# Starting the expert loop on three token tiles while the last tile's rows are finished

## The chip, the cores and the metric

The kernel runs on one core of a Trainium2 chip. The metric is the device time of one execution in microseconds, the median over several runs. The engines are TensorE (PE), VectorE (DVE), ScalarE (ACT), GpSimd (POOL) and SyncE (SP), which here only issues DMAs.

## The reference

The input is x, 32 sequences of 56 tokens and 128 channels, with a context of 32 x 1500 x 128. The block has two residual parts:

```python
x = x + tanh(g_xattn) * attention(layernorm(x), ctx)      # 16 heads of depth 8, softmax over 1500 keys
x = x + tanh(g_ffn)   * ffn(layernorm(x))

# ffn, T = 1792 tokens, 160 experts with 64 inner channels
probs   = sigmoid(x @ router_w.T + expert_bias)
top_w   = top_k(probs, 8); top_w = 2.5 * top_w / (sum(top_w) + 1e-9)
combine = zeros(T, 160) with top_w at the chosen experts
h1      = silu(einsum('th,eih->eti', x, w_gate))
routed  = einsum('eti,ehi->th', h1 * combine.T[:, :, None], w_down)
shared  = silu(x @ w_gate_shared.T) @ w_down_shared.T
ffn     = routed + shared
```

Every expert is computed for every token, and the combine weights (zero for experts not chosen) are multiplied in.

## The kernel before

**Layout.** A row of 112 tokens (PT) is the same position of two sequences; there are 16 such rows (NP). Four rows make a token tile of 448 tokens (TC), and there are four tiles (NTC). Two experts form a pair of 128 inner channels; there are 80 pairs (EP).

**Attention.** It runs over 32 batches in software-pipelined steps of 12 slots. Step s works on the keys of batch s, the maxima of batch s-1, the scores and the value products of batches s-2 and s-3, and finishes batch s-3. Slots, step numbers and named places (TOKENS_AT, LOGITS_AT, COMBT_AT and so on) order the work by hand, and each engine executes its own list in order. SyncE issues the context loads, the transposing DMAs, the stacking of keys (L387) and the row q_st (L405). GpSimd splits the context into a high and a low half-precision part (L495, L497), makes q_blk (L585) and q_st (L603), and prepares two or three expert pairs per step: load (L468 twice, L470), split (L512 to L516), store to w_scratch (L518). The 80 pairs are done when attention ends. When two batches are through, TensorE multiplies by the output weights (L1263) and VectorE adds the result to one row of xt (L1007). So the rows become ready one by one, and the last one only behind the last batch.

**Router.** Rows 0 to 11 are normalised on GpSimd in step 32, transposed, and multiplied by the router weights while attention ends. ScalarE applies one sigmoid to them (L723), VectorE finds the eight largest and clears them in a copy (L981, L984), and forms the combine weights (L988 to L994) for all twelve rows. TensorE transposes them (L1320), VectorE copies them (L959), SyncE stores them to c_scratch (L428) and reads them back, spread over 64 partitions for each expert of a pair (L421). For the last four rows, the tile 3, the same is done after the last batch, with nothing of the expert loop beside it but the shared expert's up products and the first pair's.

**Expert loop.** For each pair and tile: three up products of high and low parts (L1340), silu (L778), a product with the combine weights (L1066, "weighing"), the high part (L784), the low part (L1072) and three down products (L1368) into an accumulating bank. YB are the four banks that accumulate, ZB the four that take up products. ScalarE's order is silu of a unit, then the high part of the unit before it; VectorE's is weighing of a unit, then the low part of the unit before it; TensorE's is the down product of the unit four back (the same tile), then the up product. The intermediate values are h_f, h_hi and h_lo with a place for each tile, and s_act with two places. Expert weights (w_ring, by a transposing DMA, L439) and combine weights (c_ring) are rings of four pairs. The first four pairs are written out, the others run in a loop of 19 turns. The end (L802, L1391, L1090) transposes back, adds the residual and stores.

## Time and profile before

| | us |
|---|---|
| median of 3 runs | 1140.1 |
| lowest and highest | 1139.61, 1145.44 |
| profiled execution, its own time | 1140.58 |
| its span | 1139.1 |
| PE, DVE, ACT, POOL busy | 1069.6, 969.8, 845.1, 610.7 |

The profile lists the busy time of each engine, and for each group of instructions what ended the idle time before it. The timeline views give the start of an instruction in microseconds from the span's start, its duration, engine, line, operation and the tiles it writes and reads; in square brackets stands the idle time of its engine just before it and what ended it. "SPq" is the issuing of DMAs by SyncE. "issue" means that the profile shows nothing that was waited for. The windows view gives busy times in stretches of the span, with the clock granted to TensorE as a share of full speed (1.00 is 2.4 GHz, 0.50 is 1.2 GHz), the DMA engines' busy share and what they moved.

### The profile page before, as it was taken

What the parts mean: (1) busy time and instruction counts of PE and PEld (TensorE: products, weight loads), DVE (VectorE), ACT (ScalarE), POOL (GpSimd) and SP (SyncE); (2) the same over time, 40 slices, a digit from 0 to 9 for tenths busy, and PEclk for the clock granted to TensorE, in tenths of its full rate; (3) what the DMA queues carried; (4) which work ended last, traced back from release to release, by engine and by line L of the source; (5) the groups of instructions that cost most, each with busy time, mean ns of one, the idle gap of its engine ahead of it and who ended that gap; (6) DMA issues with size and microseconds to landing.
All of it is one profiled execution on the core that took longest, in us unless ns stands there. A gap on an engine that the chain in (4) does not pass through costs nothing.

```text
span 1139.1 us, 37969 instructions
## 1 busy us (share of the span) xinstructions
PE 1069.6 (94%) x12090; PEld 708.6 (62%) x12090; DVE 969.8 (85%) x1706; ACT 845.1 (74%) x1812; POOL 610.7 (54%) x1042
## 2 busy tenths in 40 slices
PE   2798899999999999999999999879999999999998
PEld 1366677777777777777777777644555555555554
DVE  3677788888888888888888888669999999999998
ACT  2566577777777777767777776658888888888886
POOL 4887888888888888888888988000000000000000
PEclk9799999999999999999999999889999999999999
DMA  6786866757667767568577552146777767776673
GB/s 129 162 179 150 187 155 171 170 137 182 154 143 184 156 161 176 135 159 180 139 182 164 132 144 61 25 138 209 231 226 232 239 227 226 234 236 226 225 240 115
DMA packets 201816, 197.06 MB, mean 173 GB/s; under 512 B 161999, under 2 KB 168207, under 8 KB 201782
## 3 DMA queue, kind: packets, MB, share of 16 engines
q1 hardware_dynamic: 188292, 174.14, 58.2%
q0 software_dynamic: 11520, 20.99, 6.5%
q10 hardware_dynamic: 1970, 1.49, 0.7%
q8 instruction: 18, 0.29, 0.1%
q14 instruction: 16, 0.13, 0.0%
HBM read 109.96 MB, written 12.55 MB: 108 GB/s over the span
## 4 chain that ended last, share of the span: by engine, by line
PE 45%; POOL 21%; issue 16%; DVE 9%; SPq 3%; DMA 2%; POOLq 2%; ACT 1%; DVEq 0%; ACTq 0%
PE bank L1368 15%; PE bank L1340 15%; PE bank L1170 4%; PE bank L1184 4%; DVE part_max L897 3%; POOL ctx_parts L495 3%; PE bank L1203 3%; POOL q_st L603 3%; POOL q_blk L585 3%; POOL w_in L468 3%; POOL w_in L470 2%; POOL w_out L516 2%; POOL w_out L515 2%; DVE rec L1024 2%; PE bank L1239 2%
## 5 line engine op out<-in xcount | busy, mean ns | idle before, releaser
L701 ACT ACTIVATE p_exp<-bank 125x448 f32<-125x448 f32 x768 | 400.2, 544 | 193.4 <-PE bank L1184 192.4
L897 DVE TENSOR_REDUCE part_max<-bank 128x1 f32<-128x500 f32 x672 | 420.9, 672 | 71.6 <-PE bank L1203 71.2
L1184 PE MATMUL bank<-q_st,k_stk 97*125 97x224 f16 x1536 | 275.6, 264 | 15.5 <-DMA q_st<-neg_row 8.9
L1203 PE MATMUL bank<-kparts,q_blk 128*128 128x500 f16 x672 | 256.3, 385 | 13.4 <-DVE part_max L897 11.2
L1184 PEld LDWEIGHTS bank<-q_st,k_stk 97*125 97x125 f16 x1536 | 197.2, 139 | 80.3 <-ACT p_exp L701 16.4
L1368 PE MATMUL bank<-ctT,w_ring 128*128 128x448 f16 x960 | 234.0, 353 | 3.0 <-DVE ctT L1072 3.0
L778 ACT ACTIVATE ctT<-bank 128x448 f32<-128x448 f32 x320 | 173.6, 543 | 40.6 <-PE bank L1340 16.1
L1072 DVE TENSOR_TENSOR ctT<-k_stk,ctT 128x448 f16<-128x448 f32 x320 | 198.2, 619 | 0.5 <-ACT ctT L784 0.4
L1170 PE MATMUL bank<-p_exp,v_sb 125*25 125x168 f32 (+1 forms) x6144 | 187.9, 263 | 0.4 <-ACT p_exp L701 0.4
L784 ACT ACTIVATE ctT<-k_stk 128x448 f16<-128x448 f32 x320 | 181.7, 568 | 5.5 <-DVE k_stk L1066 3.2
L1340 PE MATMUL bank<-q_hi,w_ring 128*128 128x448 f16 x640 | 174.0, 354 | 2.4 <-ACT k_stk L767 2.4
L1170 PEld LDWEIGHTS bank<-p_exp,v_sb 125*25 125x25 f32 x6144 | 142.9, 104 | 43.5 <-issue 0.6
L1066 DVE TENSOR_TENSOR k_stk<-v_sb,ctT 128x448 f32<-128x448 f32 x240 | 149.6, 624 | 8.3 <-DMA v_sb<-c_scratch 3.3
L1368 PEld LDWEIGHTS bank<-ctT,w_ring 128*128 128x128 f16 x960 | 91.5, 97 | 93.3 <-DVE ctT L1072 22.8
L497 POOL TENSOR_TENSOR ctx_parts<-ctx_in,ctx_parts 128x512 f16<-128x512 f32 x96 | 112.6, 1172 | 8.0
L1340 PE MATMUL bank<-q_lo,w_ring 128*128 128x448 f16 x320 | 113.0, 353 | 0.0
L1340 PEld LDWEIGHTS bank<-q_hi,w_ring 128*128 128x128 f16 x640 | 62.5, 98 | 61.8 <-issue 2.6
L1015 DVE SCALAR_TENSOR_TENSOR kparts<-bank,bkc,kparts 128x500 f16<-128x500 f32 x93 | 68.1, 732 | 36.3 <-ACT kparts L756 36.3
L1203 PEld LDWEIGHTS bank<-kparts,q_blk 128*128 128x128 f16 x672 | 64.8, 97 | 39.1 <-DVE part_max L897 20.3
L468 POOL DMA_DIRECT2D w_in<-in_L_ffn_w_gate_dram x160 | 85.8, 537 | 5.7
L1239 PE MATMUL bank<-wv_hi,ctT 128*125 128x128 f16 x768 | 85.0, 225 | 0.0
L1239 PEld LDWEIGHTS bank<-wv_hi,ctT 128*125 128x125 f16 x768 | 78.7, 142 | 2.9 <-issue 2.8
(157 smaller groups left out, 1241.1 us busy)
## 6 DMA issues: line engine op xcount, KB each, us to landing
v_sb<-c_scratch SPq DMA_DIRECT2D x114, 448.0 KB, 4.0
k_stk<-kparts SPq DMA_DIRECT2D x384, 93.8 KB, 3.5
ctx_in<-in_ctx_dram SPq DMA_DIRECT2D x30, 672.0 KB
k_stk<-c_scratch SPq DMA_DIRECT2D x38, 448.0 KB, 3.9
w_scratch<-w_out POOLq DMA_DIRECT2D x80, 128.0 KB, 3.2
w_in<-in_L_ffn_w_gate_dram POOLq DMA_DIRECT2D x160, 32.0 KB, 3.3
w_in<-in_L_ffn_w_down_dram POOLq DMA_DIRECT2D x80, 64.0 KB, 3.4
ctx_in<-in_ctx_dram SPq DMA_DIRECT2D x30, 78.0 KB
```

The source lines that it names most:

```text
L701: act.activation(p_exp[0:KP, j % PR, f * 448:(f + 1) * 448], ST[f][0:KP, 0:448], ACT.Exp).then_inc(exp_done, 1)
L778: act.activation(s_act[:, t % 2, :], ZB[t][:, 0:TC], ACT.Silu).then_inc(s_done, 1)
L784: act.activation(h_hi[:, t, :], h_f[:, t, :], ACT.Copy).then_inc(hh_done, 1)
L897: v.reduce_max(part_max[:, i // NCH, i % NCH:i % NCH + 1], SM[i % NSM][:, 0:CK], axis=AX.X).then_inc(sm_maxed, 1)
L1066: v.tensor_tensor(h_f[:, t, :], c_ring[q][:, t * TC:(t + 1) * TC], s_act[:, t % 2, :], ALU.mult).then_inc(h_done, 1)
L1072: v.tensor_tensor(h_lo[:, t, :], h_f[:, t, :], h_hi[:, t, :], ALU.subtract).then_inc(hl_done, 1)
L1170: last = pe.matmul(OB[32 * (g % 4):32 * (g % 4) + VW, at:at + w], v_sb[0:KP, u, j, g, 0:VW], p_exp[0:KP, j % PR, src:src + w], start=(j == ...
L1184: last = pe.matmul(ST[f][0:KP, (g % 2) * GC:(g % 2 + 1) * GC], k_stk[0:97, u, g, j * KP:(j + 1) * KP], q_st[0:97, u, g, :, :].rearrange("p ...
L1203: pe.matmul(SM[i % NSM][:, 0:CK], rows, kparts[:, u, 0, c * CK:(c + 1) * CK], start=True, stop=True).then_inc(sm_done, 1)
L1239: last = pe.matmul(VB[0:KP, i * D:(i + 1) * D], ctT[:, u, c, part, i, 0:KP], w[:, :], start=(n == 0), stop=(n == 2))
L1340: last = pe.matmul(ZB[t][:, 0:TC], w_ring[:, q, a, :], xparts[b][:, t * TC:(t + 1) * TC], start=(j == 0), stop=(j == 2))
L1368: last = pe.matmul(YB[t][:, 0:TC], w, hparts[b][rows, t, :], start=(shared and i == 0), stop=(end and i == 2), skip_group_check=True)
```

## The change

Units are numbered k in the order in which they are started. The first three are the shared expert for tiles 0 to 2. Then come 24 units: eight expert pairs (AHEAD) for tiles 0 to 2 (TS is 3). Unit 27 (TAIL) is the shared expert of tile 3, and units 28 to 35 are the same eight pairs for tile 3. From unit 36 on the order is as before, from pair 8.

In the 27 first units h_f, h_hi, h_lo and the up banks have three places in use, and GpSimd makes the low parts in place of VectorE. In between, at fixed unit numbers, stands what was done for tile 3 before: the last residual row behind unit 5, three Newton steps on VectorE in place of ScalarE's root, the scaling, tokens at 12, logits at 15, sigmoid, the eight largest, the weights, and their transposes at 24. The last batch's spread and output products move from the last attention step into this list.

The router's work for tiles 0 to 2 is done tile by tile: searches and sums on VectorE, the subtraction and the product with the sum's inverse on GpSimd. TensorE gets twelve products without use (keep_busy) where ScalarE computes the sigmoid. SyncE loads the eight pairs' expert weights (w_ahead) before the combine weights; it stores and reads back the combine weights tile by tile (two pairs per DMA for the first four pairs), and tile 3's for all eight pairs by two DMAs (c_last). c_ring is laid out by tile, so a load writes four pieces to each partition. h_f lies in xnT. The gate matrices of a pair are loaded by one DMA in place of two, and the early normalisation has three Newton rounds in place of four. YB, ZB, TOKB, LGB and CTB get other banks.

```diff
+    AHEAD, TS = 8, NTC - 1
+    TAIL = TS + TS * AHEAD
+    OUT_LATE, TOKENS_LATE, LOGITS_LATE, COMBT_LATE = 5, 12, 15, 24
...
+        c_last = e_words[:, 0:AHEAD * TC].rearrange("p (n c) -> p n c", c=TC)
...
-        YB = [bank[0], bank[1], bank[2], bank[3]]
-        ZB = [bank[4], bank[5], bank[6], bank[7]]
+        YB = [bank[0], bank[1], bank[5], bank[4]]
+        ZB = [bank[7], bank[2], bank[3], bank[6]]
...
+        def earlier(k):
+            if k < TS or k == TAIL:
+                return 0
+            return k - TS + 1 if k < TAIL else k - NTC + 1
...  SyncE
+            def store(c):
+                sp.wait_ge(cb_cp, 2 * c + 2)
+                sp.dma_start(c_scratch[:, :, c * TC:(c + 1) * TC], combT[0:EP, :, c * TC:(c + 1) * TC]).then_inc(c_stored, 16)
+                sp.wait_ge(c_stored, 16 * (c + 1))
...
+            for n in range(AHEAD):
...
+                sp.dma_start_transpose(w_ahead[n], w_scratch[n].rearrange("p b c -> p (b c)")).then_inc(w_first, 16)
...
+            for t in range(TS):
+                store(t)
+                for j in range(2):
+                    for a in range(2):
+                        src = c_scratch[2 * j:2 * j + 2, a, t * TC:(t + 1) * TC].unsqueeze(0).to_broadcast([I, 2, TC])
+                        sp.dma_start(c_pairs[j][a::2, t, :, :], src).then_inc(c_first[t], 16)
...
+            for n in range(WR, AHEAD):
+                sp.wait_ge(h_done, TS * (n - WR) + TS)
+                weights_of(n, n % WR, TS)
+            store(TS)
+            sp.wait_ge(pv_done, B * KT)
+            for a in range(2):
+                src = c_scratch[0:AHEAD, a, TS * TC:N].unsqueeze(0).to_broadcast([I, AHEAD, TC])
+                sp.dma_start(c_last[a::2, :, :], src).then_inc(c_late, 16)
...  GpSimd
             def load_pair(h, i):
-                for a in range(2):
-                    pool.dma_start(w_in[a::2, i, 0, :], gate_pairs[bass.ds(h * WPP + i, 1), a].rearrange("a p c -> p (a c)"))\
-                        .then_inc(w_here[i], 16)
+                pool.dma_start(w_in[:, i, 0, :], gate_pairs[bass.ds(h * WPP + i, 1)].rearrange("a e p c -> p (a e) c"))\
+                    .then_inc(w_here[i], 16)
...
+            for k in range(TAIL):
+                b = k % TS
+                rows = slice(0, I if k < TS else 128)
+                pool.wait_ge(hh_done, k + 1)
+                until(pool, dn_done, earlier(k))
+                pool.tensor_tensor(h_lo[rows, b, :], h_f[rows, b, :], h_hi[rows, b, :], ALU.subtract).then_inc(hl_done, 1)
...  ScalarE
+            for k in range(TS, TAIL):
+                silu(k, k % TS, weighed(k))
+                if k > TS:
+                    hi_part(k - 1, (k - 1) % TS, weighed(k - 1), earlier(k - 1))
+                if k == TOKENS_LATE + 1:
+                    tokens(TS)
+                if k == LOGITS_LATE + 3:
+                    sigmoid(2, *LATE)
...  VectorE, behind the eight pairs
+            dve.wait_ge(c_late, 32)
+            for k in range(TAIL + 1, TAIL + 1 + AHEAD):
+                weigh(k, place(k), weighed(k), c_last[:, k - TAIL - 1, :])
+                lo_part(k - 1, place(k - 1), I if k - 1 == TAIL else 128)
...  TensorE
+            def keep_busy():
+                pe.wait_ge(lg_biased, 2)
+                for _ in range(WARM):
+                    pe.matmul(bank[2][0:I, 0:TC], sg[:, 0, :], q_hi[:, 0:TC], start=True, stop=True)
...
+            for n in range(1, AHEAD):
+                for t in range(TS):
+                    k = TS + TS * n + t
+                    down(k - TS, t, t, w_ahead[n - 1])
+                    up(k, t, t, w_ahead[n])
+                    if k == TOKENS_LATE:
+                        tokens(TS)
+                    if k == LOGITS_LATE:
+                        logits((4, 5))
+                    if k == COMBT_LATE:
+                        weights_out(TS)
+            pe.wait_ge(cb_cp, 2 * NTC)
+            shared_up(TS)
```

## Rows read from the trace of the kernel before

**Rows 1.** Windows: stretch, its length, busy us (instructions) of each engine.
```profile
720.00:730.00 10.00, 9.27 (x89) 6.38 (x90) 5.22 (x31) 5.45 (x12) 0.00 (x0) 0.50 0.10 23
...
745.00:772.00 27.00, 18.57 (x76) 10.11 (x76) 17.39 (x49) 12.17 (x22) 0.00 (x0) 0.81 0.42 132
747.00:756.00 9.00, 7.41 (x30) 4.83 (x29) 4.44 (x16) 2.03 (x3) 0.00 (x0) 0.69 0.90 300
772.00:1130.00 358.00, 357.40 (x1888) 182.52 (x1889) 351.94 (x632) 317.80 (x631) 0.00 (x0) 1.00 0.69 224
```
The engines are PE, PE's weight loads, DVE, ACT and POOL; then follow the granted clock, the DMA engines' share and GB/s.

**Rows 2.** Timeline of TensorE, two of its waits in attention.
```profile
131.28 0.40 PE L1184 MATMUL bank<-q_st,k_stk 97*125 97x224 f16 x2 [3.03 <-DMA q_st<-neg_row]
...
508.09 0.40 PE L1184 MATMUL bank<-q_st,k_stk 97*125 97x224 f16 x2 [1.08 <-DMA q_st<-neg_row]
```

**Rows 3.** Timeline of GpSimd in attention.
```profile
379.63 1.67 POOL L585 TENSOR_TENSOR q_blk<-q_hi,head_mask 128x896 f16<-128x896 f16 x1
...
392.25 1.12 POOL L468 DMA_DIRECT2D w_in<-in_L_ffn_w_gate_dram  x2
393.37 0.71 POOL L470 DMA_DIRECT2D w_in<-in_L_ffn_w_down_dram  x1
...
420.91 1.67 POOL L585 TENSOR_TENSOR q_blk<-q_hi,head_mask 128x896 f16<-128x896 f16 x1
...
471.84 0.71 POOL L470 DMA_DIRECT2D w_in<-in_L_ffn_w_down_dram  x1 [2.34 <-issue]
...
473.25 1.16 POOL L497 TENSOR_TENSOR ctx_parts<-ctx_in,ctx_parts 128x512 f16<-128x512 f32 x1
```

**Rows 4.** Timeline of VectorE: o_nrm, once in each step.
```profile
432.28 0.39 DVE L1028 TENSOR_TENSOR o_nrm<-rec,o_raw 128x224 f32<-128x224 f32 x1
...
473.62 1.04 DVE L1028 TENSOR_TENSOR o_nrm<-rec,o_raw 128x224 f32<-128x224 f32 x1
...
516.90 0.65 DVE L1028 TENSOR_TENSOR o_nrm<-rec,o_raw 128x224 f32<-128x224 f32 x1
```

**Rows 5.** Timeline of all engines late in the expert loop.
```profile
1122.08 0.73 PE L1368 MATMUL bank<-ctT,w_ring 128*128 128x448 f16 x3
...
1122.28 0.54 ACT L778 ACTIVATE ctT<-bank 128x448 f32<-128x448 f32 x1
...
1122.72 0.57 ACT L784 ACTIVATE ctT<-k_stk 128x448 f16<-128x448 f32 x1
...
1122.97 0.62 DVE L1066 TENSOR_TENSOR k_stk<-v_sb,ctT 128x448 f32<-128x448 f32 x1
1123.03 0.35 PE L1340 MATMUL bank<-q_lo,w_ring 128*128 128x448 f16 x1
```

**Rows 6.** Timeline of ScalarE and TensorE at the end of attention.
```profile
715.17 1.28 ACT L723 ACT_TABLE_LOAD   x1
...
720.18 1.07 PE L1184 MATMUL bank<-q_st,k_stk 97*125 97x224 f16 x4 [3.67 <-ACT p_exp L701]
...
742.83 0.59 PE L1170 MATMUL bank<-p_exp,v_sb 125*25 125x168 f32 x16 [0.36 <-ACT p_exp L701]
```

**Rows 7.** DMA issues: engine, count, KB each, median us to landing.
```profile
v_sb<-c_scratch SPq DMA_DIRECT2D x6, 336.0 KB, 5.3
c_scratch<-q_stk SPq DMA_DIRECT2D x4, 280.0 KB, 3.0
...
v_sb<-c_scratch SPq DMA_DIRECT2D x6, 112.0 KB, 2.8
```

**Rows 8.** Timelines of SyncE, VectorE and TensorE before the dense stretch.
```profile
745.32 3.76 SPq L421 DMA_DIRECT2D v_sb<-c_scratch  x6
...
763.56 1.14 DVE L959 COPY q_stk<-bank 80x448 f32<-80x448 f32 x2
...
771.16 0.63 DVE L1066 TENSOR_TENSOR k_stk<-v_sb,ctT 128x448 f32<-128x448 f32 x1 [3.25 <-DMA v_sb<-c_scratch]
...
772.38 0.74 PE L1368 MATMUL bank<-ctT,w_ring 128*128 128x448 f16 x3 [2.80 <-DVE ctT L1072]
```

465 lines of the change are left out of this document (268 added, 197 removed).

## The prediction, made before the result was known

> **What bounds the kernel now.** I read four views in this order. First the busy time by stretches [rows 1]. The reader is to see that from 772 to 1130 us TensorE is busy 357.4 of 358.0 us at a granted clock of 1.00: the expert loop is bound by TensorE. From 745 to 772 it is busy only 18.6 of 27 us, at 0.81. The change aims at this second stretch, and at what lies just ahead of it.
>
> Then the timelines, to find which wait ends last at the edges. In the attention loop TensorE has three waits for the row of q_st, of which the first and the last stand in [rows 2]. That row is sent only when GpSimd has made q_st. GpSimd [rows 3] never idles there: from one q_blk to the same one two steps later it takes 41.28 us (379.63 to 420.91). TensorE's own two steps take 41.34 (432.28 to 473.62 in [rows 4]). So GpSimd has almost no slack. When its DMA issue hangs for 2.34 us at 471.84, the next two steps take 43.28 us instead of 41.34.
>
> The expert loop deals in units: the up product, silu, weighing, hi part, lo part and down product of one token tile for one expert pair. There are 324 (80 pairs and the shared expert, times four tiles). One costs TensorE six products. At 772.4 [rows 8] 316 are left, and the stretch to 1130.5 gives 1.133 us each [rows 1]. So I count units: the change is worth what it finishes before the dense stretch, less what it adds.
>
> **1. Attention loop: one gate DMA for two.** For each expert pair two issues of together 1.12 us become one of 128 rows. It costs between 0.56 (one of the two) and 0.71 us (the down matrices' issue, also over 128 partitions) [rows 3]. GpSimd gains 0.41 to 0.56 per expert pair, 2.0 to 2.8 per two steps, so the hangs of about 2.3 us are swallowed. These cost 1.9 us at 473.62 to 516.90 [rows 4] and about 1.1 at the one before. In the first wait of [rows 2] the three expert pairs ahead of it give 1.7, and the two before them let the preceding step begin 0.4 earlier: 2.1 of 3.03 us go, and with them the half clock from 132.8 to 136, worth 1.6. Sum 6.6; I take **-6.0**. The bounds are -7.5 (all three waits and the clock) and -3.0 (hangs only). TensorE is otherwise busy, so nothing more comes. One Newton round less saves GpSimd four small operations that nobody waits for: 0.
>
> **2. Last steps of attention.** Probabilities need two table loads of 1.28 us, TensorE idles 3.67 us, and then runs at half clock from 720 to 730 [rows 1, 6]. Twelve added products of 0.19 us fill 2.3 us of that idle time, for nothing, since they end before the scores' banks are freed. At full clock the stretch would be bound by ScalarE's exponentials. I take **-2.4** (bounds 0, if the clock falls all the same, and -4.6, half of the 9.27 us busy). The router's two long products leave VectorE for idle GpSimd; VectorE's searches are the same in number. The last value product ends about 741.0 instead of 743.4 [rows 6].
>
> **3. Start of the eight pairs.** SyncE handles the tiles one after another: store (3.0 us to landing), wait, four loads at 0.63 each [rows 7, 8]: 5.5 us, and the issue of the store. From about 731.3 these rounds put the loads of tile 2 at 745.3 to 747.8, and they land near 750.7. The units of tiles 0 and 1 don't need them; the first weighing of tile 2 waits until 750.7. Its w_ahead transposes stand before 727 and are hidden. Without this wait TensorE would be ready about 748, so 2 to 3 us hang on it.
>
> **4. Rate of the eight pairs.** Here I see the main cost. With three tiles a ring closes: an up product, silu of k, then hi of k-1 (behind silu of k on ScalarE), lo of k-1 on GpSimd, its down product, and the up product of k+2. From [rows 5]: 0.04 to silu, 1.01 for silu and hi, 1.30 from the start of a down to the end of the up behind it. GpSimd's subtraction of 512 columns takes 1.16 [rows 3]; 448 columns are about 1.03. With 0.08 for each of two handovers the ring is 0.04 + 1.01 + 0.08 + 1.03 + 0.08 + 1.30 = 3.54 us for two units: **1.77 per unit**, not 1.133. Bounds: 1.133 (TensorE alone) and 2.35 (the same ring with TensorE's 1.30 at half clock).
>
> VectorE's late work (row 15, Newton, tokens, logits, top 8) lies in the slack of about 1 us per unit; I charge only the burst behind the first tile-2 unit. ScalarE's sigmoid with two table loads of 1.28 [rows 6] is about 3.3 us, less 0.75 of slack; for TensorE's logits and transposes I estimate 0.9. The up product of unit 8 ends at 754.4 and that of unit 11 at 760.4; fourteen units at 1.77 and the 3.5 extra give 788.7 for unit 25.
>
> The SBUF lock is the skill's rule against this part. At 473.62 o_nrm, two SBUF inputs, takes 1.04 instead of 0.39 us and ends with GpSimd's subtraction that began at 473.25 [rows 3, 4]. The Trainium skill (SBUF — State Buffer, Who interferes with whom) says that a VectorE instruction with two SBUF inputs and a GpSimd one that reads SBUF exclude each other. By it weighing (0.62) and lo would be in series, but in this ring lo starts when weighing ends, so it would add 0.05 per unit, about 1 us in all, plus 1 or 2 where a late product gets in first.
>
> **5. Tile 3 catches up.** The wait of before for tile 3's weights (3.25 us, [rows 8]) comes back larger. VectorE's two copies of the transposed weights (1.14, [rows 8]) end about 790.9. Then the store, 3.1 with its issue; then two loads of 8 x 448 words to 64 partitions each, 1.83 MB. Loads ran at 300 GB/s in 747 to 756 [rows 1], 6.1 us for these, and took 1.7 from the issue at 745.3 [rows 8] to the first bytes: 7.8 (bounds 5.3, one 336 KB load [rows 7], and 10). They land at 801.8. Only units 26 and 28 to 30 are in flight meanwhile: TensorE stops at about 795. Queued behind the waiting weighing of unit 28 is the lo part of unit 27, and for that waits down 27. It starts 1.2 later, at **803.0**.
>
> By the Trainium skill (DMA: Bandwidth & Descriptors, Anatomy of one DMA), 2.0 us plus bytes over 436 GB/s, an estimate for these loads would be 6.2 instead of 7.8, and the sum 1.6 lower; the trace's rate is the lower one.
>
> **6. Dense stretch.** At 803.0, when down 27 starts, 297 downs and 293 ups remain, 295 units. Before, at 772.4, there were 318 and 314, 316 units. The end moves by 803.0 - 772.4 - 21 x 1.133 = **+6.8**. After 8 us of idleness the clock will be low at the restart, as it was at 720: I take 3.4 us at half rate, **+1.7** (bounds 0 and 4.6). The loads of the combine weights now write four pieces of 1792 bytes instead of one of 7168; the nearest rows are small and large loads of before, at 2.8 and 5.3 us [rows 7], while a slot is refilled some three pairs (13.6 us) ahead: 0, hidden by TensorE, and up to +10 if DMA became the bound, which I hold unlikely. New banks: 0, none is shared by two streams.
>
> **Sum.** On the clock of the profile parts 2 to 5 are inside the 803.0. So 1140.58 + 6.8 + 1.7 - 6.0 = 1143.1 for the profiled execution, which stood 0.5 above the median of 1140.1 (its span is 1139.1, 1.5 lies outside). I predict **1142.5**, no difference that can be told: a measurement of this kernel tells 0.5% (5.7 us) from none.
>
> **The rivals.** (a) *TensorE, not the ring, paces the eight pairs.* If silu, hi and lo hide as in the four-tile loop, the 17 units from 8 to 25 save 0.64 each, 10.9 us, and the time is 1142.5 - 10.9 = 1131.6. For it: in [rows 5] every handover is 0.04 to 0.1, and matmul ends are modelled. Against it: the order on ScalarE and a GpSimd subtraction nearly twice VectorE's 0.62. A part of it (1.5 per unit) and the short end of the loads would already give 1136.
>
> (b) *The clock falls in the eight pairs* (slower). In the ring TensorE is busy 1.13 of 1.77, 64%. For it: 745 to 772 was granted 0.81 at 18.6 of 27 us, 69% busy [rows 1]. Against: gaps of 0.6 us are short beside the 3.67 ahead of 720. At half clock throughout the unit is 2.35, 17 x 0.58 = +9.9: 1152.4. It decides if more than a third of that stretch is at half clock.
>
> (c) *The merged gate DMA changes nothing*, because TensorE's waits have another cause (the row's own DMA): +6.0, 1148.5. For it: the releaser named in [rows 2] is a DMA. Against: that DMA is issued right behind q_st.
>
> **How the numbers follow.** As worked out 0.42, (a) in whole or part 0.30, (b) 0.15, (c) 0.13. The first gives no difference in 0.34 and a faster or slower kernel in 0.04 each, its own range is 1136 to 1149. (a) is faster in 0.27 and the same in 0.03; (b) and (c) are slower in 0.25, the same in 0.03. So faster 0.31, same 0.40, slower 0.29. The range, 1130 to 1153, reaches to (a) and (b) whole; about 0.15 is left out.
>
> **What would show it.** Part 1: no wait for q_st's row at 131, 299 and 508, two steps at 41.3 throughout, GpSimd with idle time. Part 2: PEclk 1.0 from 720 to 745. Part 4: downs 1.77 apart between the first and the last of the eight pairs. Part 5: a wait of VectorE for the weights of tile 3 of 8 to 10 us, TensorE idle 8, a low clock behind it. Part 6: from the end of the wait to the end 295 x 1.133 us. I am wrong if the eight pairs run near 1.3 per unit, or if the stall on tile 3's weights is under 4 us.

## The result: slower by 1.5%, outside the range

| | before | after |
|---|---|---|
| median, us | 1139.9 (4 runs) | 1157.9 (4 runs) |
| lowest and highest | 1139.51, 1145.44 | 1156.26, 1159.31 |
| ratio, with its 95% interval | | 1.0149 [1.0129, 1.0169] |
| profiled execution, its span | 1140.58, 1139.1 | 1156.67, 1155.1 |

The forecast was 1142.5, in a range of 1130 to 1153: 15.4 us too low. In the profiled executions the miss is 13.6 (1156.67 against the sum of 1143.1). Line numbers below are those of the changed kernel: L1301 value products, L1490 up, L1500 down, L1157 weighing, L1166 and L672 lo on VectorE and GpSimd, L831 hi, L825 silu, L1110 o_nrm.

The windows of the profile after (same columns as [rows 1]) show at once where the time is not:

```profile
738.00:749.00 11.00, 8.12 (x43) 3.96 (x41) 4.19 (x5) 6.24 (x13) 4.89 (x5) 1.00 0.37 119
749.00:762.00 13.00, 7.52 (x20) 2.58 (x21) 7.29 (x22) 2.82 (x6) 3.65 (x4) 0.51 0.62 165
762.00:783.00 21.00, 15.84 (x78) 7.19 (x76) 10.38 (x18) 14.10 (x26) 10.76 (x10) 0.98 0.31 99
783.00:790.00 7.00, 5.32 (x14) 1.92 (x15) 5.14 (x20) 3.04 (x8) 3.51 (x3) 0.52 0.00 0
790.00:800.00 10.00, 6.66 (x36) 3.19 (x35) 7.10 (x9) 5.10 (x11) 5.76 (x5) 1.00 0.00 0
800.00:815.00 15.00, 7.67 (x32) 3.21 (x31) 4.46 (x8) 4.86 (x11) 1.29 (x2) 0.77 0.87 309
815.00:1130.00 315.00, 315.00 (x1667) 162.69 (x1665) 309.88 (x555) 280.15 (x556) 0.00 (x0) 1.00 0.77 224
```

From 815 TensorE is full, as it was from 772 before. The loss lies between 738 and 815: 77 us in which TensorE is busy for 51.1, part of it at half clock. A summary of waits over this stretch (engine, line, what it waited for, us in total, times, longest) names the places:

```profile
DVE xnT L1157 <- ACT ctT L825: 13.4, 9, 3.7
DVE xnT L1157 <- DMA p_exp<-c_scratch: 9.9, 1, 9.9
DVE xnT L1157 <- DMA k_stk<-c_scratch: 9.3, 2, 5.9
...
PE bank L1500 <- POOL ctT L672: 14.4, 12, 4.1
PE bank L1500 <- DVE ctT L1166: 7.3, 1, 7.3
```

The waits for DMAs are those for the weights of tiles 1 and 2 (k_stk from c_scratch, 3.3 and 5.9 us) and of tile 3 (p_exp); the others belong to the ring of three tiles and to what gets in its way. Cut at the events that the prediction had placed:

| stretch | forecast | after | off |
|---|---|---|---|
| to the last value product | 735.0 | 737.75 | +2.75 |
| from there to the first weighing of tile 2 (753.46) | 9.7 | 15.7 | +6.0 |
| from there to the end of up(25) (796.57) | 38.0 | 43.1 | +5.1 |
| from there to down 27 (810.53) | 14.3 | 14.0 | -0.3 |
| from there to the end | 344.6 | 344.6 | 0.0 |

(The forecast's 803.0 for down 27 and the times ahead of it are moved by its -6.0 of part 1.) The first row flatters the forecast: TensorE's first wait, for the loaded Wo, happened to be 3.4 us shorter in this execution than in that of before (10.87 and 14.29). Without that, parts 1 and 2 missed by some 6 us, not 2.75.

**Tile 2's weights.** SyncE's queue: start, duration of the issue, what is issued.

```profile
728.96 0.69 SPq L446 DMA_DIRECT2D c_scratch<-q_stk  x1
732.00 1.38 SPq L464 DMA_DIRECT2D v_sb<-c_scratch  x2
...
734.72 0.64 SPq L446 DMA_DIRECT2D c_scratch<-q_stk  x1
741.07 1.27 SPq L464 DMA_DIRECT2D v_sb<-c_scratch  x2
...
743.68 0.62 SPq L446 DMA_DIRECT2D c_scratch<-q_stk  x1
747.67 1.26 SPq L464 DMA_DIRECT2D v_sb<-c_scratch  x2
```

Each first load is issued when the store before it has landed. The stores took 3.04, **6.35** and 3.99 us, where I had taken 3.0 from [rows 7] for all three. The two late ones were issued right behind four loads; in [rows 7] the stores had no load ahead of them. Eight further kernels below have the same chain of stores: their first store took 3.0 to 3.1 us, the second 3.9 to 6.0, the third 3.8 to 4.1. So a store behind loads always took longer, and 6.35 was the longest of nine. From the first store's issue to the first weighing of tile 2 it is 24.5 us (728.96 to 753.46) where the forecast had 19.4 (731.3 to 750.7): 5.1 of the 6.0.

**VectorE held up.** Timeline rows of VectorE, GpSimd and TensorE at the end of attention, and of VectorE in the eight pairs:

```profile
719.51 1.53 POOL L663 TENSOR_TENSOR ctx_in<-kparts,ctx_in 112x640 f32<-112x640 f32 x1 [0.76 <-DVE ctx_in L1057]
719.56 1.51 DVE L1063 TENSOR_SCALAR wsum<-wsum 112x4 f32<-112x4 f32 x1
721.39 0.39 DVE L982 COPY o_raw<-bank 128x224 f32<-128x224 f32 x1
...
721.93 1.52 PE L1301 MATMUL bank<-p_exp,v_sb 125*25 125x168 f32 x24 [2.35 <-DVE o_raw L982]
...
758.29 0.99 DVE L1130 TENSOR_TENSOR lst<-lst 112x4 f32<-112x4 f32 x1
...
761.03 0.15 DVE L1130 TENSOR_TENSOR lst<-lst 112x4 f32<-112x4 f32 x1
```

An addition to four numbers a row took 1.51 us (1.51 or 1.52 in each of the three tiles; before the change such additions took 0.17), and ended when GpSimd's subtraction of 640 columns did. The two rows of L1130 are the same instruction, a product of four numbers a row in row 15's Newton steps, once beside GpSimd's lo and once not: 0.99 and 0.15. Two of row 15's later pieces were held up in the same way: its scalings (L1137) took 1.31 us for two, and the subtraction for its combine weights (L1145) 1.68. In e10 and e13 below, where GpSimd makes no lo there, the three take 0.15, 0.60 and 0.82. TensorE's wait at 721.93 is the third in that chain.

**The ring.** TensorE's down products where nothing late is in the way:

```profile
763.98 0.74 PE L1500 MATMUL bank<-ctT,ctx_parts 128*128 128x448 f16 x3 [0.53 <-POOL ctT L672]
...
765.75 0.74 PE L1500 MATMUL bank<-ctT,ctx_parts 128*128 128x448 f16 x3 [0.46 <-POOL ctT L672]
```

They are 1.77 us apart, as forecast, and so are the next three. ScalarE then loads the sigmoid's table and silu's again, and TensorE finds itself at half clock behind it:

```profile
779.16 1.28 ACT L783 ACT_TABLE_LOAD   x1
...
781.21 1.28 ACT L825 ACT_TABLE_LOAD   x1
...
784.68 1.30 PE L1500 MATMUL bank<-ctT,ctx_parts 128*128 128x448 f16 x3 [3.03 <-POOL ctT L672]
```

**Tile 3** waits nearly as forecast (9.9 us of VectorE, 7.33 of TensorE; the same wait before is in [rows 8]):

```profile
801.89 1.29 SPq L477 DMA_DIRECT2D p_exp<-c_scratch  x2
...
809.32 0.63 DVE L1157 TENSOR_TENSOR xnT<-p_exp,ctT 128x448 f32<-128x448 f32 x1 [9.91 <-DMA p_exp<-c_scratch]
...
810.53 1.30 PE L1500 MATMUL bank<-ctT,sd 64*128 64x448 f16 x3 [7.33 <-DVE ctT L1166]
```

### The profile page after: what moved, and what is told of

Same layout as the page of the kernel before. It is cut to its first block, busy times and chain, and to the rows that moved or that the text cites. A ratio compares the mean times of both kernels' runs of the same rounds, so it can differ in the third digit from the quotient of the medians.

```text
span 1155.1 us, 37333 instructions
## 1 busy us (share of the span) xinstructions
PE 1072.5 (93%) x12102; PEld 708.9 (61%) x12102; DVE 965.2 (84%) x1695; ACT 845.5 (73%) x1810; POOL 613.2 (53%) x991
## 4 chain that ended last, share of the span: by engine, by line
PE 73%; DVE 11%; issue 5%; SPq 4%; POOL 3%; DMA 3%; ACT 1%; DVEq 0%; POOLq 0%
PE bank L1500 15%; PE bank L1490 15%; PE bank L1301 11%; PE bank L1334 10%; PE bank L1315 10%; DVE part_max L968 6%; PE bank L1370 4%; PE bank L1358 4%; DVE rec L1106 3%; POOL ctT L672 1%; PE bank L1413 1%; SPq L412 1%; SPq L367 1%; DMA ctx_in<-in_ctx_dram 1%; SPq L359 1%
## 5 line engine op out<-in xcount | busy, mean ns | idle before, releaser
L825 ACT ACTIVATE ctT<-bank 128x448 f32<-128x448 f32 x320 | 173.9, 544 | 57.0 <-PE bank L1490 24.0
L1500 PE MATMUL bank<-ctT,w_ring 128*128 128x448 f16 x864 | 210.6, 352 | 0.1
L831 ACT ACTIVATE ctT<-xnT 128x448 f16<-128x448 f32 x320 | 182.1, 569 | 20.2 <-DVE xnT L1157 17.7
L1301 PE MATMUL bank<-p_exp,v_sb 125*25 125x168 f32 (+1 forms) x6144 | 186.7, 262 | 2.3 <-DVE o_raw L982 2.3
L1166 DVE TENSOR_TENSOR ctT<-xnT,ctT 128x448 f16<-128x448 f32 (+1 forms) x297 | 183.7, 619 | 0.1
L1301 PEld LDWEIGHTS bank<-p_exp,v_sb 125*25 125x25 f32 x6144 | 142.5, 104 | 44.6 <-issue 2.5
L1490 PE MATMUL bank<-q_hi,w_ring 128*128 128x448 f16 x576 | 156.0, 352 | 0.0
L1500 PEld LDWEIGHTS bank<-ctT,w_ring 128*128 128x128 f16 x864 | 84.3, 98 | 79.1 <-DVE ctT L1166 3.8
L1157 DVE TENSOR_TENSOR xnT<-v_sb,ctT 128x448 f32<-128x448 f32 x156 | 97.2, 623 | 20.6 <-DMA k_stk<-c_scratch 9.3
L1157 DVE TENSOR_TENSOR xnT<-k_stk,ctT 128x448 f32<-128x448 f32 x156 | 98.1, 629 | 8.9 <-ACT ctT L825 5.6
L1490 PE MATMUL bank<-q_lo,w_ring 128*128 128x448 f16 x288 | 101.5, 352 | 0.0
L1097 DVE SCALAR_TENSOR_TENSOR kparts<-bank,bkc,kparts 128x500 f16<-128x500 f32 x93 | 68.0, 731 | 35.8 <-ACT kparts L816 35.8
L1334 PEld LDWEIGHTS bank<-kparts,q_blk 128*128 128x128 f16 x672 | 65.0, 97 | 41.3 <-DVE part_max L968 22.8
L1490 PEld LDWEIGHTS bank<-q_hi,w_ring 128*128 128x128 f16 x576 | 56.4, 98 | 52.7
```

The lines of the kernel that those rows point to most:

```text
L825: act.activation(s_act[:, (b if isinstance(r, int) is False else r - 1) % 2, :], ZB[b][:, 0:TC], ACT.Silu)\
L831: act.activation(h_hi[:, b, :], h_f[:, b, :], ACT.Copy).then_inc(hh_done, 1)
L1157: v.tensor_tensor(h_f[:, b, :], c, s_act[:, (b if isinstance(r, int) is False else r - 1) % 2, :], ALU.mult).then_inc(h_done, 1)
L1166: v.tensor_tensor(h_lo[0:rows, b, :], h_f[0:rows, b, :], h_hi[0:rows, b, :], ALU.subtract).then_inc(hl_done, 1)
L1301: last = pe.matmul(OB[32 * (g % 4):32 * (g % 4) + VW, at:at + w], v_sb[0:KP, u, j, g, 0:VW], p_exp[0:KP, j % PR, src:src + w], start=(j == ...
L1334: pe.matmul(SM[i % NSM][:, 0:CK], rows, kparts[:, u, 0, c * CK:(c + 1) * CK], start=True, stop=True).then_inc(sm_done, 1)
```

## The experiments

Each is timed as a ratio to the kernel before on the same chip; the changed kernel's is 1.0149. The intervals are some 0.2% to 0.4% to either side, so a difference of two ratios below 3 us (5 us for e9) is not settled by them, and the traces carry it. They are compared by three stretches, since executions of the same code already start differently: TensorE's first wait, for the loaded Wo, was 14.3 us in the profiled execution of before, 10.9 in that of after and 10.9 to 15.0 over all runs. OB is the bank in which the value products of attention add up; VectorE copies it once for each batch (o_raw<-bank). The columns are: from the last copy of OB to the first weighing of tile 2; from there to the first weighing of tile 3; from there to the end.

| kernel | ratio [95%] | copy to tile 2 | tile 2 to tile 3 | to the end |
|---|---|---|---|---|
| after | 1.0149 [1.0129, 1.0169] | 15.6 | 55.9 | 345.8 |
| e1_sums_first | 1.0138 [1.0102, 1.0175] | 15.6 | 56.3 | 346.0 |
| e4_store_queue | 1.0122 [1.0098, 1.0145] | 11.9 | 56.0 | 346.3 |
| e5_hi_first | 1.0176 [1.0149, 1.0203] | 14.6 | 58.9 | 346.9 |
| e6_two_loads | 1.0159 [1.0133, 1.0185] | 12.9 | 53.6 | 346.3 |
| e9_up_first | 1.0110 [1.0068, 1.0151] | 15.5 | 49.5 | 345.6 |
| e10_up_first_lo_vector | 1.0127 [1.0092, 1.0162] | 14.8 | 50.1 | 346.3 |
| e14_no_table | 1.0111 [1.0094, 1.0128] | 14.8 | 52.2 | 346.8 |
| e15_short_chain | 1.0072 [1.0055, 1.0089] | 13.9 | 49.0 | 344.3 |
| e12_all_lo_gpsimd | 0.9972 [0.9954, 0.9991] | 10.4 | 43.7 | 344.5 |
| e13_all_lo_vector | 0.9997 [0.9983, 1.0010] | 10.7 | 45.5 | 344.4 |
| f2_all_phase | 0.9995 [0.9983, 1.0006] | 10.2 | 43.5 | 344.0 |
| f3_no_busy | 1.0176 [1.0156, 1.0196] | 14.2 | 55.1 | 345.6 |

The second column repeats to within 1.2 us where the code in it is the same (55.1 to 56.3); the first does not (12.9 to 15.6), so a gain in it under 3 us is not shown. Most of that spread is the landing of tile 1's store: 3.9 us in e6, which has 12.9, and 6.35, 6.0 and 5.5 in after, e1 and e9, which have 15.5 to 15.6.

### e1_sums_first

```diff
-                then(pool.tensor_tensor(comb[:, p, :], prob[:, p, :], comb[:, p, :], ALU.subtract))
                 pool.wait_ge(sums_done, c + 1)
+                then(pool.tensor_tensor(comb[:, p, :], prob[:, p, :], comb[:, p, :], ALU.subtract))
```

> The changed kernel, but GpSimd waits for VectorE's sums before its first product of the combine weights (prob minus comb), not between its two products. Theory (the GpSimd product shuts out VectorE's small operation): the three 112x4 additions of VectorE's sums, 1.51 to 1.52 us each in the changed kernel against 0.17 before the change, go back to about 0.2; the copy of OB at 721.4 starts about 1.3 us earlier, TensorE's wait of 2.35 us at 721.9 shrinks to about 1 and the half clock behind it goes; the last value product ends 1.5 to 3 us earlier than 737.75, and the time falls by as much, from 1157.9 to 1155 to 1156.5. Rival (the small additions are long because the semaphore of the chain arrives late, or by another engine's traffic): they stay at 1.5 us and the time does not move. A second rival: GpSimd's product, now later, meets the next VectorE operation instead (search or copy), which then takes 1.2 to 1.5 us: same total.

Measured: 1157.75 us, ratio 1.0138. The additions in its trace:

```profile
717.50 0.17 DVE L1063 TENSOR_SCALAR wsum<-wsum 112x4 f32<-112x4 f32 x1
...
720.28 0.84 DVE L1063 TENSOR_SCALAR wsum<-wsum 112x4 f32<-112x4 f32 x1
```

The first is at 0.17; the other two (0.84 and, at 724.05, 0.54) now meet the end of GpSimd's second product of the tile before. So the product did hold the addition up. From o_nrm at 701.3 to the copy of OB at 721.5 it is 20.1 us against 22.1 in after: 2.0 us gained. (This stretch repeats: 22.1 in every variant of the changed kernel with the old order, 20.1 in every one with the new.) TensorE's wait of 2.35 is gone, but from the one copy of OB to the next it takes 18.2 instead of 16.4, because half clock lasted from 718 to 728 where it had been 722 to 725. (Other kernels with after's code show 16.5 to 17.8 here, so this is in part chance.) No gain in time is shown. The mechanism held; that the clock would give more on top was wrong.

### e4_store_queue

```diff
             for t in range(TS):
-                store(t)
+                if t == 0:
+                    store(t)
+                else:
+                    sp.wait_ge(c_stored2[t - 1], 16)
                 for j in range(2):
...
             for k in range(TS):
+                if k < TS - 1:
+                    act.wait_ge(cb_cp, 2 * k + 4)
+                    act.dma_start(c_scratch[:, :, (k + 1) * TC:(k + 2) * TC], combT[0:EP, :, (k + 1) * TC:(k + 2) * TC])\
+                       .then_inc(c_stored2[k], 16)
                 shared(k, k)
```

> The changed kernel, but the stores of the combine weights of tiles 1 and 2 are issued by ScalarE, behind its last exponential, in a queue of its own; SyncE only waits for them before the loads. Theory (the second and third store stand in SyncE's queue behind the loads of the tile before, and SyncE waits out each landing): the store of tile 1, 6.35 us from issue to landing in the changed kernel, takes about 3; the loads of tile 2 are issued by about 740 instead of 750.2, the wait of 5.93 us that VectorE has before the first tile-2 weighing (753.5) goes, this weighing starts near 748, and TensorE's low clock from 749 to 762 shortens. Time 4 to 7 us under the changed kernel's 1157.9, about 1152. Rival (the loads themselves set the time, their landing takes as long wherever the stores are): first tile-2 weighing within 1 us of 753.5, no gain. Second rival (the gain is given back at tile 3): the ring of the eight pairs starts 5 us earlier, but the late work of row 15 does not, and the wait for tile 3's weights grows by the same: time as it was.

Measured: 1155.5 us, ratio 1.0122. ScalarE's issues, and VectorE's first weighing of tile 2:

```profile
738.86 0.72 ACTq L849 DMA_DIRECT2D c_scratch<-q_stk  x1
...
741.77 0.59 ACTq L849 DMA_DIRECT2D c_scratch<-q_stk  x1
...
752.47 0.62 DVE L1165 TENSOR_TENSOR xnT<-v_sb,ctT 128x448 f32<-128x448 f32 x1 [2.39 <-DMA k_stk<-c_scratch]
```

Tile 1's store stands behind ScalarE's last exponentials and is issued at 738.9, not 734.7; it took 4.5 to landing and landed later than in after. Tile 2's landed by 745.9, and then all loads followed one another. The wait of 5.9 for tile 2 became 2.4. That is 3.7 us in the table's first column against after and 1.0 against the shortest of the same code, and none in the second: the rounds are a cost of their own, smaller than I expected from this way of mending it. And a queue of its own did not bring the store back to 3 us while loads were under way: 4.5 here, 5.3 in e12 below. That speaks for the transfers under way, and not only for its place in SyncE's queue; no run takes the two apart.

### e5_hi_first

```diff
             for k in range(TS, TAIL):
-                silu(k, k % TS, weighed(k))
                 if k > TS:
                     hi_part(k - 1, (k - 1) % TS, weighed(k - 1), earlier(k - 1))
+                silu(k, k % TS, weighed(k))
```

> The changed kernel, but in the loop of three tiles over eight pairs ScalarE makes the hi part of unit k-1 before silu of unit k, not behind it. Ring theory: the ring was silu and hi (1.01), GpSimd's lo (1.03), down and up (1.30) and the handovers, 3.54 us for two units, 1.77 each. In the new order one unit's own chain is up, silu 0.5, weighing 0.62, hi 0.5, lo 1.03, down and up 1.30 and handovers, 4.28 us for three units, 1.43 each. Down products 1.4 to 1.5 apart where they were 1.77, 17 units save 0.34 each: 5 to 6 us, less what the late burst on VectorE holds: the time falls from 1157.9 to 1152 to 1154. Rival (GpSimd and VectorE exclude each other on two SBUF inputs, so weighing 0.62 and lo 1.03 are in series at 1.65 us a unit whatever ScalarE's order): 1.65 to 1.7 per unit, a gain of 1 to 2 us. Second rival (TensorE's clock sets the rate): it stays at 1.77.

Measured: 1161.0 us, ratio 1.0176. The intervals touch, but the middle stretch is 3.0 us longer than in after. A unit took 2.20 us, and one turn of the ring reads (hi, lo, weighing, next hi):

```profile
771.71 0.58 ACT L831 ACTIVATE ctT<-xnT 128x448 f16<-128x448 f32 x1 [1.19 <-DVE xnT L1157]
...
772.36 1.04 POOL L672 TENSOR_TENSOR ctT<-xnT,ctT 128x448 f16<-128x448 f32 x1 [1.17 <-ACT ctT L831]
...
772.75 1.13 DVE L1157 TENSOR_TENSOR xnT<-k_stk,ctT 128x448 f32<-128x448 f32 x1 [1.07 <-ACT ctT L825]
...
773.91 0.58 ACT L831 ACTIVATE ctT<-xnT 128x448 f16<-128x448 f32 x1 [0.76 <-DVE xnT L1157]
```

The weighing starts at 772.75, lasts 1.13 instead of 0.62 and ends half a microsecond behind GpSimd's lo (773.40). The next hi needs it. So hi, lo and weighing form a ring although no semaphore joins lo to weighing. Without the hold-up the ring of hi, silu and weighing would be 1.7 us: my expectation of 1.43 had missed that ring too. Both my theory and its figure fell; the lock, given there as the first rival at 1.65 to 1.7, is real and costlier than I had put it.

### e6_two_loads

```diff
-            for a in range(2):
-                src = c_scratch[0:AHEAD, a, TS * TC:N].unsqueeze(0).to_broadcast([I, AHEAD, TC])
-                sp.dma_start(c_last[a::2, :, :], src).then_inc(c_late, 16)
+            for s, n0 in ((c_late, 0), (c_late2, AHEAD // 2)):
+                for a in range(2):
+                    src = c_scratch[n0:n0 + AHEAD // 2, a, TS * TC:N].unsqueeze(0).to_broadcast([I, AHEAD // 2, TC])
+                    sp.dma_start(c_last[a::2, n0:n0 + AHEAD // 2, :], src).then_inc(s, 16)
```

> The changed kernel, but tile 3's combine weights for the eight pairs are loaded in two halves (four pairs each, a semaphore each), and VectorE waits for the second half only before the fifth of its eight units. Theory (the stall of the catching-up tile is store, fixed time of a DMA, and bytes at some 300 GB/s): the first half lands 3.0 us earlier, 4.8 us behind the issue instead of 7.4; VectorE's wait of 9.9 us shrinks to about 7, TensorE's of 7.3 to about 4.5; time 2.5 to 4 us under 1157.9. Rival (the time to landing is mostly fixed, or halves of one queue share the engines): under 1 us. A wait for the second half may come back four units later: it has 3 x 1.13 us and the first unit to land in, so at most 1 us.

Measured: 1157.9 us, ratio 1.0159: no gain by the times; 2.3 us in the middle stretch of the trace. In its trace VectorE's wait is 7.80 where it was 9.91, and TensorE's 5.22 where it was 7.33:

```profile
806.96 0.62 DVE L1158 TENSOR_TENSOR xnT<-p_exp,ctT 128x448 f32<-128x448 f32 x1 [7.80 <-DMA p_exp<-c_scratch]
...
808.16 1.30 PE L1503 MATMUL bank<-ctT,sd 64*128 64x448 f16 x3 [5.22 <-DVE ctT L1167]
```

Halving the bytes saved 2.1 of 7.4 us from issue to landing, not 3.0, and half clock behind the wait stays. The stall is more fixed time than I had counted.

### e2_gate_only and e3_busy_only

The kernel before, with one part of the change alone. The first is the diff's load_pair and its count of 32 (part 1 of the prediction); the second adds twelve products (part 2):

```diff
+            def keep_busy():
+                pe.wait_ge(lg_biased, 2)
+                for _ in range(WARM):
+                    pe.matmul(bank[2][0:I, 0:TC], sg[:, 0, :], q_hi[:, 0:TC], start=True, stop=True)
```

> The kernel before the change with one part alone: the gate matrices of an expert pair come in one DMA of 128 rows, not in two of 64. The prediction gave this part -6.0 us (bounds -7.5 and -3.0). The trace of the changed kernel speaks for less: the early o_nrm came 5.0 us sooner (136.65 against 141.68), but the last value product only 5.6 sooner with another part in it, and two steps take 41.65 us throughout. Theory: the gain is made before 160 us and at the one hang, and a toll of 0.3 us per two steps (every second o_nrm takes 0.7 instead of 0.39 us and holds up the maxima behind it) gives part of it back over 13 pairs of steps: 1 to 3 us faster than before. Rival (the prediction as it stood): two steps at 41.34 throughout and 6 us faster. Second rival: nothing, because the early stretch differs from run to run by as much.

Measured: 1138.8 us in 10 runs, ratio 0.9981 [0.9963, 1.0000], that is -2.2 us (-4.2 to 0) for a forecast of -6.0. GpSimd's hangs no longer stop TensorE, but two steps take 41.65 to 41.7 us nearly throughout instead of 41.34. An o_nrm of every second step in its trace (those between take 0.39):

```profile
513.30 0.75 DVE L1027 TENSOR_TENSOR o_nrm<-rec,o_raw 128x224 f32<-128x224 f32 x1
```

From the third o_nrm (141.7 before, 137.7 here) to the one near 700 it takes 563.6 us, and 562.8 before: this toll of 0.3 us per two steps cancels what the hangs gave. What is left is the early stretch, 4.0 us, and 2.6 of these are TensorE's shorter first wait for Wo (11.65 for 14.29). The other traces agree. With the merged DMA the third o_nrm comes 0.9 to 3.9 us earlier behind that wait than before, and from there to the one near 700 it takes 562.3 to 563.6 us (565.9 in f2), against 562.8 and 563.3 in the two kernels without it.

> The kernel before the change with one part alone: twelve added products of TensorE behind the last early logits, while ScalarE makes the probabilities. The prediction gave -2.4 us for the clock from 720 to 730. Theory now: the granted clock still falls to 0.5, only later or earlier by a few us, as it did in the three last variants of the changed kernel (718 to 728 at 0.5 with these products in), because TensorE is slack in this stretch, not only idle once: time within 1 us of before. Rival (the prediction): PEclk 1.0 throughout 716 to 740 and 2 to 3 us faster.

Measured: 1140.9 us in 10 runs, ratio 1.0011 [0.9993, 1.0029]: no gain. Its windows:

```profile
720.00:730.00 10.00, 8.98 (x162) 6.08 (x160) 8.24 (x27) 7.00 (x16) 0.00 (x0) 1.00 0.03 6
...
766.00:774.00 8.00, 6.67 (x20) 2.82 (x21) 5.62 (x10) 3.71 (x8) 0.00 (x0) 0.57 0.42 99
```

The profile looks as the rival said, and the time is the theory's: full clock from 720 to 730 as in the prediction, and from o_nrm at 703.0 to the last copy of OB 35.8 us instead of 39.0. But from that copy to the end it takes 398.1 instead of 395.6: here the clock was low from 766 to 773, where the same window of before shows 1.00. (Before was low earlier, 0.58 from 760 to 764, where e3 shows 1.00.)

### e9_up_first and e10_up_first_lo_vector

```diff
                     k = TS + TS * n + t
-                    down(k - TS, t, t, w_ahead[n - 1])
                     up(k, t, t, w_ahead[n])
+                    down(k - TS, t, t, w_ahead[n - 1])
```

> The changed kernel, but in the loop of three tiles TensorE issues the up product of unit k before the down product of unit k-3, so that an up no longer waits behind a down for the lo part. This takes the up product out of the ring that I counted: up, silu, hi, lo, down would then close over three units, 3.54 / 3 = 1.18 us. Lock theory (GpSimd's lo, 1.03, and VectorE's weighing, 0.54 to 0.62, shut each other out, as in the run with hi first, where weighing took 1.12 us and a unit 2.20): they are in series, at least 1.65 us a unit whatever TensorE's order; down products 1.65 to 1.7 apart, the time 1 to 3 us under 1157.9. Rival (no lock, the ring alone): 1.2 to 1.3 per unit where VectorE has no late work, 8 to 10 us under 1157.9.

Measured: 1152.5 us, ratio 1.0110; tile 2 to tile 3 takes 49.5 instead of 55.9. The ring of TensorE is out of the way, and GpSimd and VectorE alternate (both rows are groups of instructions without idle time in between):

```profile
769.03 3.37 DVE L1157 TENSOR_TENSOR xnT<-k_stk,ctT 128x448 f32<-128x448 f32 x3
...
769.28 5.01 POOL L672 TENSOR_TENSOR ctT<-xnT,ctT 128x448 f16<-128x448 f32 x4 [1.30 <-PE bank L1500]
```

Three weighings in 3.37 us are 1.12 each, four lo parts in 5.01 are 1.25 each, where alone they take 0.62 and 1.03. The gain lies between theory and rival: the two engines hold each other up, but one lo and one weighing did not take the 1.65 us in series that I had expected.

The second kernel has this and the lo parts of the routed units on VectorE:

```diff
-            for k in range(TAIL):
+            for k in range(TS):
...
                     weigh(k, t, weighed(k), c_ring[n % WR][:, t, :])
+                    if k == TS + 1:
+                        dve.wait_ge(hl_done, TS)
+                    if k > TS:
+                        lo_part(k - 1, (k - 1) % TS)
```

> As the run before (up product ahead of the down product in the loop of three tiles), and the lo part of the routed units made by VectorE, as in the dense loop, so that GpSimd has nothing there. Lock theory: without GpSimd's products no weighing is held up, VectorE paces the loop at 1.12 to 1.2 us a unit where it has no late work, and the late work of row 15 (about 10 us on VectorE by its rows in the changed kernel) adds to it: 24 units in 37 to 39 us instead of 43, 4 to 6 us under 1157.9. TensorE at 1.13 of 1.2 us a unit should also keep its clock. Rival (the late chain on VectorE becomes the bound, since every piece of it now waits behind two products a unit, so that tile 3's weights come as late as before): stall for tile 3's weights longer by what the loop gained, time 1156 to 1159.

Measured: 1153.8 us, ratio 1.0127; 50.1 us in the middle stretch, wait for tile 3's weights 8.5. What VectorE gains by being free of GpSimd's products it gives back by making the lo parts itself.

### e14_no_table and e15_short_chain

```diff
-                act.activation(prob[:, p0:p1, :], prob[:, p0:p1, :], ACT.Sigmoid).then_inc(prob_done, 1)
+                act.activation(prob[:, p0:p1, :], prob[:, p0:p1, :], ACT.Sigmoid if n == 1 else ACT.Silu).then_inc(prob_done, 1)
```

> The changed kernel, but the late sigmoid (tile 3's probabilities, in the middle of the eight pairs) is replaced by Silu, whose table is loaded already: this leaves out the sigmoid of the last four rows of tokens, so their routing is another. Theory: the two table loads of 779.2 to 782.5 and TensorE's wait of 3.0 us at 784.7 go, and so does the half clock from 784 to 790; everything behind it, the late chain too, is earlier by 3.0 to 3.7 us for the wait and 1 to 2 for the clock: 1157.9 falls to 1153 to 1154. Rival (the ring has slack of 0.6 us a unit, so the stall is made up, or the wait for tile 3's weights grows by it): within 1 us of 1157.9.

Measured: 1153.2 us, ratio 1.0111, 4.3 us less than after by the ratios; in the traces the middle stretch is 3.7 shorter. The half clock of 783 to 790 is gone (1.00 here and in 786 to 792):

```profile
780.00:786.00 6.00, 4.22 (x22) 1.65 (x20) 4.38 (x16) 4.20 (x9) 3.35 (x4) 1.00 0.00 0
```

The theory held, in size too: two table loads in the ring, with the half clock behind them, cost the whole 3.7, not the loads less the slack.

```diff
-    OUT_LATE, TOKENS_LATE, LOGITS_LATE, COMBT_LATE = 5, 12, 15, 24
+    OUT_LATE, TOKENS_LATE, LOGITS_LATE, COMBT_LATE = 5, 11, 13, 20
...
-                if k == LOGITS_LATE + 3:
+                if k == LOGITS_LATE + 2:
                     sigmoid(2, *LATE)
```

and on VectorE the searches one unit earlier, with the sums in the same unit.

> The changed kernel with the late chain of tile 3 packed closer: tokens behind unit 11 (12 before), logits behind 13 (15), sigmoid one unit earlier after them, searches and sums in one unit, so that the transposes of its combine weights stand behind unit 20 and no longer 24. Theory: the store and the loads for tile 3 are issued 4 units of 1.77, some 7 us, earlier, while the same units still run; VectorE's wait for them falls from 9.9 to 3 to 4 us and TensorE's stall of 7.3 to about 1, its half clock with it: 6 to 8 us under 1157.9. Rival (VectorE's late work bunched into fewer units stretches the ring by as much, since every piece also meets GpSimd's lo): 0 to 3 us under it.

Measured: 1148.7 us, ratio 1.0072, 8.8 us less than after. VectorE's wait for tile 3's weights:

```profile
805.67 0.63 DVE L1157 TENSOR_TENSOR xnT<-p_exp,ctT 128x448 f32<-128x448 f32 x1 [2.72 <-DMA p_exp<-c_scratch]
```

TensorE waits 0.51 us at the down behind it, and the half clock at the restart goes as well (345.8 to 344.3 in the last column). It is the largest single cause, and a matter of placement alone: the unit behind which the last tile's transposes stand.

### e12_all_lo_gpsimd and e13_all_lo_vector

The edits of e1, e6, e9 and e15, and the stores mended better than in e4: those of tiles 0 and 1 go out together on SyncE, and ScalarE issues only tile 2's, whose transposes move from (B + 2, 2) to (B + 2, 0):

```diff
-            for t in range(TS):
-                store(t)
+            for t in range(2):
+                sp.wait_ge(cb_cp, 2 * t + 2)
+                sp.dma_start(c_scratch[:, :, t * TC:(t + 1) * TC], combT[0:EP, :, t * TC:(t + 1) * TC])\
+                  .then_inc(c_stored3[t], 16)
+            for t in range(TS):
+                sp.wait_ge(c_stored3[t], 16)
```

> All in one: up product ahead of down, stores of tiles 0 and 1 issued together and that of tile 2 from ScalarE's queue with its transposes one slot earlier, tile 3's weights in two loads, GpSimd's product of the combine weights behind VectorE's sums, late chain packed closer. If the causes found are separate and add (up first -5.4 as measured; stores -2.4; two loads about -2 by the traces; packed chain -5; sums 0 to -1), the time is 1143 and the last wait for tile 3's weights is under 3 us. If they overlap (the packed chain and the two loads remove the same stall), 1147. If the lock between GpSimd's lo and VectorE is what remains, the loop of eight pairs still takes 1.6 us a unit in its trace.

Measured: **1136.0 us** in 7 runs, ratio 0.9972 [0.9954, 0.9991]: faster than the kernel before by 0.28%, and 20 us faster than after by the ratios. It was better than I had expected. Its window of the eight pairs, and from VectorE's timeline the first weighing of tile 3 (that of tile 2 is at 746.33):

```profile
746.00:786.00 40.00, 29.49 (x137) 13.26 (x136) 30.98 (x67) 24.10 (x44) 22.93 (x20) 0.91 0.30 87
```

```profile
790.04 0.62 DVE L1166 TENSOR_TENSOR xnT<-p_exp,ctT 128x448 f32<-128x448 f32 x1 [2.46 <-DMA p_exp<-c_scratch]
```

TensorE is still busy only 29.5 of 40 us. From the last copy of OB to the end it takes 398.6 us where the kernel before takes 395.6: the eight pairs are still no gain in themselves. That this kernel beats the one before must come from ahead of that copy (735.9 against 743.5; 2.9 of these 7.6 us are TensorE's shorter wait at the very start).

> As the run with all in one, with the lo parts of the routed units on VectorE. Theory: with the loads of tile 2 in time and no GpSimd product, VectorE alone paces the eight pairs, 24 weighings and los at 1.12 us and some 10 us of late work, 37 us in all; 0 to 3 us faster than the same with lo on GpSimd, 1141 to 1144. Rival: as before between those two (1152.5 and 1153.8), no difference, because the late chain waits for VectorE either way.

Measured: 1140.0 us in 10 runs, ratio 0.9997 [0.9983, 1.0010]: no faster than before, and 2.9 us slower by the ratios than with lo on GpSimd, with intervals that just overlap. The theory fell. It had 37 us for the 24 units; from the first weighing of tile 2 to that of tile 3, two units fewer, it takes 45.5. VectorE is busy 35.9 of the 46 us from 748 to 794, so its load alone does not pace the loop; that TensorE's waits there end with VectorE's lo (7.3 us in 7 waits) speaks for the order of its work, which no run tried.

### f1_gate_phase, f2_all_phase, f3_no_busy

```diff
+                early = not isinstance(step[0], int) and step[1] == 1
                 for c in range(NCH):
+                    if early and c == NCH - 1:
+                        queries_of(step)
                     if on(step, -1):
                         split_ctx(back(step, -1), c)
```

(queries_of makes q_st, which otherwise stands behind the loop.)

> The kernel before with the merged gate DMA (which gave -2.2 us alone, forecast -6.0), and in every odd step of the attention loop GpSimd makes q_st before its last context split, not behind it. Theory: with GpSimd ahead, the end of that split and q_st fall on VectorE's o_nrm (0.72 instead of 0.39 us in every second step), which holds up the maxima; two steps take 41.65 instead of 41.34 us, 13 pairs of steps, some 4 us. Moved, o_nrm takes 0.4 in both steps, two steps take 41.35, and the kernel is 4 us faster than with the merged gate alone: 1134 to 1136. Rival (two steps are 41.65 for another cause, as the maxima's own banks, and o_nrm only shows it): o_nrm short, two steps still 41.6, no gain. Second rival (the moved product meets another VectorE operation with two SBUF inputs): no gain, another operation long.

Measured: 1140.4 us in 12 runs, ratio 0.9998 [0.9987, 1.0010]. Two steps take 41.38 us, as expected, in most of the loop. But twice it loses more than the toll was: 0.74 us near 305, and 1.78 near 514, where GpSimd runs a little late and o_nrm falls 0.2 us behind the start of its four products of q_st, not ahead of them. Near 514:

```profile
513.36 2.14 POOL L609 TENSOR_TENSOR q_st<-q_stk,stack_mask 96x224 f16<-96x224 f16 x4
...
513.56 2.20 DVE L1034 TENSOR_TENSOR o_nrm<-rec,o_raw 128x224 f32<-128x224 f32 x1
```

From the third o_nrm to the one near 700 it takes 563.1 us, against 563.6 with the merged gate alone. The toll was what I said (o_nrm is down to 0.43 us); taking it away by phase exposes the loop to a larger one. It is not always the full one: near 305 o_nrm also began 0.2 us behind the four products (305.71 and 305.92) and took 1.17 us.

> The kernel with all mends in one (1136.0 us), with the same move of q_st in the odd steps of the attention loop. Theory: 4 us faster, about 1132 to 1133, that is 0.6 to 0.7% faster than the kernel before. Rival: 1136.

Measured: 1139.7 us in 12 runs, ratio 0.9995 [0.9983, 1.0006]: 2.6 us slower than e12_all_lo_gpsimd by the ratios, and 3.1 in the traces from the third o_nrm to the one near 700 (565.9 for 562.8). In its trace o_nrm took 2.18 and 2.20 us in two steps, and the pairs of steps around these took 44.7 and 43.1 us. The same cause.

> The changed kernel without its twelve added products of TensorE in the probabilities' wait (forecast -2.4 us for them; alone in the kernel before they gave 0.11% slower, interval -0.07 to 0.29, though the profile showed full clock from 716 to 742 us). Theory: in the changed kernel they give nothing either, since a clock that falls some 10 us later costs the same then: 1157 to 1159. Rival (the forecast): 2.4 us slower, 1160 and more, with half clock from 720 to 730.

Measured: 1160.3 us (6 runs, one of them, at 2692.5, left out of the ratio), ratio 1.0176 [1.0156, 1.0196]. Against after's 1.0149 [1.0129, 1.0169] that is 3 us slower, with intervals that overlap a little, and so nearer to the forecast's -2.4 for the added products than to my theory of nothing. Its windows from 714 to 728 have a clock of 0.54, those of after 0.88:

```profile
714.00:728.00 14.00, 12.46 (x133) 8.91 (x134) 12.76 (x44) 7.18 (x16) 8.35 (x6) 0.54 0.28 55
```

But of the thirteen kernels with the added products only e3 keeps the full clock between 700 and 740. The others are at half clock for 3.4 us (after), 6.8 (four kernels) or 10.2 (seven), 7.9 on average over all thirteen; the four without the products for 10.2 or 13.7, 12.0 on average. So the products shorten the half clock and seldom prevent it. What that is worth stays open: 0 to 3 us.

## Why the prediction was wrong

**Part 3, the start of the eight pairs, failed by +6.0.** The step "store (3.0 us to landing), wait, four loads" took every store at 3.0. With four loads issued right ahead of it, it was 6.35 and 3.99 (3.9 to 6.0 and 3.8 to 4.1 in eight other kernels). The rounds took 24.5 us instead of 19.4. The +6.0 of this execution is at the long end: the same code gave 12.9 to 15.6 us from the last copy of OB, 3 to 6 us over the forecast.

**Part 4, the rate, was right in its ring and failed in its sum by +5.1.** The ring of 3.54 us for two units is in the trace to the hundredth: from the up product of unit 11 to that of unit 19 it takes 14.18 us, 1.77 each. And e9 showed that it is the ring that it was said to be: taken out, 6.4 us go. What failed are the extras, 1.1 us up to the up product of unit 8, 1.0 from there to unit 11 and 3.0 behind it. "ScalarE's sigmoid ... about 3.3 us, less 0.75 of slack" with 0.9 for TensorE's late products, 3.5 in all, left out the half clock behind it (783 to 790); e14 puts the two table loads with that half clock at 3.7 to 4.3 us. In the trace the three units around them took 4.6 us more than the ring's, and the last three, among which TensorE waits for row 15's combine weights, 1.9 more. "I charge only the burst behind the first tile-2 unit" and "0.05 per unit, 1 in all, plus 1 or 2" were too little. Rival (b), the low clock, came in part: 0.51 from 749 to 762 and 0.52 from 783 to 790. But of the 38.3 us in which the rival's 17 units ran (758.3 to 796.6) it took 11.3, just under the third that the rival had named. That its 1152.4 was the nearest of the cases was luck: most of the miss came from the stores, the table loads and parts 1 and 2.

**The rule on the shared port was weighed too narrowly.** The traces show VectorE's addition to four numbers at 1.52 us instead of 0.17, its L1130 at 0.99 instead of 0.15, o_nrm at 2.20 instead of 0.39, each ending with GpSimd's work or up to 0.26 us behind it. The Trainium skill (SBUF — State Buffer, Who interferes with whom) names two kinds of VectorE operation that exclude GpSimd: those with two SBUF inputs and those in a two-port mode. I had counted weighings, by the first kind, and "1 or 2" for late products. The small products of row 15 are of the first kind too (L1130 has both inputs in SBUF). The additions of the sums have one input; that they ran in a two-port mode is not shown by any run, only that GpSimd held them up. Both, and the products of the combine weights that the change moves to GpSimd ("the router's two long products leave VectorE for idle GpSimd", taken as free), were not in the sum. With the ring and no hold-up e5 should have taken 1.7 a unit; it took 2.20, where hi, lo and the rest of the weighing behind it make 2.2.

**Part 1 was mis-sized: -2.2 (interval -4.2 to 0) for -6.0.** All three waits of [rows 2] were to go, and two steps were to take 41.3 throughout. The hangs are swallowed, but every second o_nrm takes 0.72 and two steps 41.65: 0.31 for each of some 13 pairs is 4.0 us. The bounds of -7.5 to -3.0 had no term for a faster GpSimd meeting VectorE elsewhere, and f1, without most of that toll, met larger ones and was no faster than before. Besides, 3.4 us of the 5.0 that lie between the traces of before and after at the third o_nrm are the wait for Wo at the very start, which differs from execution to execution. (The part's four terms, 1.9, 1.1, 2.1 and 1.6, add up to 6.7 and not 6.6, which moves nothing, as 6.0 was taken.)

**Part 2: -2.4 forecast, 0 to -3 measured, and unsettled.** Alone it showed the full clock and no gain; undone in the changed kernel it cost 3 us; and of thirteen kernels with the products one kept the full clock that the part had counted on. In parts 1 and 2 together, the last value product came 2.75 us late, in spite of the 3.4 us of luck at the start. One reason is the chain of additions, copy of OB and value product, 2.0 us up to that copy by e1.

**Part 5 and part 6 held.** Forecast 8 us of idle TensorE, measured 7.33; VectorE's wait 8 to 10, measured 9.9; 7.4 us from the issue of tile 3's loads to their first use, for 7.8 worked out from the trace's rate; half clock at the restart 1.7, measured 1.5 (345.8 against 344.3 without it); the dense stretch 344.6, measured 344.6, with its loads in four pieces at no cost, though the DMA engines' share rose from 0.69 to 0.77. (The estimate by the Trainium skill, DMA: Bandwidth & Descriptors, Anatomy of one DMA, was 6.2; the section gives its fit for DMAs issued by GpSimd, and these are SyncE's.) The large stall that I had foreseen was real but not necessary: e15 took 8.8 us off by transposes four units earlier. I had taken the late chain's places as given and never priced them.

**The sum of the causes.** Ratios taken off one at a time give 3.1 us (e4), 4.4 (e9) and 8.8 (e15), 16.3 in all; the combined kernel, which has also e1's and e6's edits, gave 20, each with an uncertainty of some 3 us. In the traces' middle stretch e9 and e15 alone give 13.3 and the combined kernel 12.2. So they are separate causes that nearly add, and e6's 2.3 is probably in the same stall as e15's. The table loads (e14, 4.3) are still in that kernel. What stays open: why the same store takes 3.9 us in one execution and 6.35 in another, why the clock falls at different places in such similar executions, and with it the worth of the added products.

## What to carry to other kernels

When work moves to an idle engine, list what it can meet there, instruction by instruction, and not only the long ones: here the cost of moving products to GpSimd was paid by VectorE's smallest operations, and through them by TensorE. In a stretch with few units in flight a delay in any stage is on the path, so first find the ring and then price each visitor to it whole, table loads and clock included. And where the last tile's chain ends in a store and a load, count backwards from the unit that needs them to the unit that starts them: moving that by four units was worth more than any other single edit here.

## What the runs showed of the hardware

- In these traces a product of GpSimd holds up VectorE's small operations on SBUF, and a row of four products can do so to the end: o_nrm that came 0.2 us behind their start took 2.20 us (f1), and 2.18 and 2.20 in f2. Once in f1 it took only 1.17 from the same position, so the wait is not always for the whole row. Where GpSimd was idle (e10, e13), the operations held up in after were short. Operations of VectorE that read a PSUM bank kept their times: the maxima 0.67 us and rec 1.56 on average, before and after.
- In e9 the two engines took turns, one weighing and one lo in about 1.25 us, less than the 1.65 that their single times (0.62 and 1.03) make in series.
- A 280 KB store issued right behind four loads of 224 KB in the same queue landed after 6.35 us (3.9 to 6.0 in eight other kernels); with nothing ahead of it, after 3.04. From ScalarE's queue, with such loads under way, it took 4.5 (e4) and 5.3 us (e12).
- An execution's very start differs by up to 4 us for the same loads (TensorE's wait for Wo 10.9 to 15.0 us over 17 traces), more than most effects studied here; single traces must be compared from a common event on.
